# One core: a product of 512 bf16 columns into an unused bank behind each step's product of a tanh recurrence

## The reference

```
def _L0_attn_b_ref(x, A, B, C, gamma, beta):
    xb = jnp.einsum('bsd,ed->sbe', x, B)
    def step(h, xb_t):
        h = jnp.tanh(h @ A.T + xb_t)
        y = h @ C.T
        return (h, y)
    h0 = jnp.zeros((batch, d), dtype=x.dtype)
    _, ys = jax.lax.scan(step, h0, xb)
    out = jnp.transpose(ys, (1, 0, 2)) + x
    mu = jnp.mean(out, axis=-1, keepdims=True)
    var = jnp.mean(jnp.square(out - mu), axis=-1, keepdims=True)
    return (out - mu) * jax.lax.rsqrt(var + LN_EPS) * gamma + beta
...
x = x + _L0_attn_b_ref(_layernorm(x, axis=-1), L0_attn_b_A, ...)
```

## Time and profile before

| | |
|---|---|
| median of 3 runs | 6355.99 us (6347.57 to 6366.04) |
| the profiled execution, its own time | 6365.01 us |
| its span, first to last instruction | 6363.1 us |
| TensorE's mean granted clock over the span | 0.891 |
| the recurrence, from the first product to the last tanh | 2491.9 to 2753.4 us of the span |

### The profile page before, as it was taken

How to read it: one execution, slowest core, us unless ns; L and a number is a source line. 1 busy time by engine, 2 the same in 40 slices (tenths; PEclk the granted TensorE clock), 3 DMA queues, 4 the chain that set the end, 5 groups by cost and what they waited for, 6 DMA issues and landing times. The chain is left out here.

```text
span 6363.1 us, 79030 instructions
## 1 busy us (share of the span) xinstructions
PE 5155.9 (81%) x22250; PEld 2583.2 (41%) x22314; DVE 4310.5 (68%) x6171; ACT 2866.6 (45%) x4845; POOL 3250.2 (51%) x2383
## 2 busy tenths in 40 slices
PE   4888888888886897778977999954897799974897
PEld 1333333333332343534433555422664344442564
DVE  4999999999998474054765777752675566652675
ACT  4665665655654354233543555521332344431232
POOL 2788888888886252023523444317333455526333
PEclk8999999999999897578988999966998899986898
DMA  1224211211211000000002333222454333302455
GB/s 71 80 99 146 102 56 78 80 55 79 80 60 53 0 0 0 0 0 0 0 7 55 87 84 83 52 81 74 159 189 139 81 90 92 90 1 72 152 187 177
DMA packets 175518, 476.34 MB, mean 75 GB/s; under 512 B 29888, under 2 KB 55232, under 8 KB 147392
## 3 DMA queue, kind: packets, MB, share of 16 engines
q1 hardware_dynamic: 156992, 434.35, 21.4%
q0 software_dynamic: 18176, 37.79, 1.7%
HBM read 364.94 MB, written 107.07 MB: 74 GB/s over the span
## 5 line engine op out<-in xcount | busy, mean ns | idle before, releaser
L337 POOL TENSOR_TENSOR mamba_bu<-mamba_du,mamba_b_all 128x1024 f32<-128x1024 f32 x512 | 1200.3, 2355 | 282.5 <-DVE mamba_hc L599 270.2
L592 DVE TENSOR_TENSOR_SCAN mamba_bu<-psum,mamba_bu 128x512 f32<-128x512 f32 x1024 | 1194.2, 1208 | 157.6 <-ACT psum L529 124.9
L428 PE MATMUL psum<-mamba_hc,consts 128*128 128x512 f32 x2048 | 1019.0, 622 | 31.7 <-DVE mamba_du L604 28.6
L529 ACT ACTIVATE psum<-mamba_delta,A 128x510 f32<-128x510 f32 x1024 | 684.6, 685 | 571.4 <-DVE mamba_bu L592 556.8
L599 DVE TENSOR_TENSOR mamba_hc<-mamba_bu,psum 128x1024 f32<-128x1024 f32 x512 | 612.9, 1197 | 6.5 <-PE psum L419 4.5
L1597 POOL DMA_INDIRECT results<-ffn_moe_y_rows,ffn_moe_row_of x312 | 302.1, 968 | 506.3 <-DVE ffn_moe_y_rows L1787 430.7
L428 PEld LDWEIGHTS psum<-mamba_hc,consts 128*128 128x128 f32 x2048 | 404.2, 199 | 371.3 <-issue 351.0
L1712 ACT ACTIVATE ffn_moe_act<-ffn_moe_act 128x512 f32<-128x512 f32 x344 | 217.0, 631 | 719.9 <-DVE ffn_moe_act L1756 719.8
L2140 POOL TENSOR_TENSOR loc_q_bd<-loc_q_max,weights_l1a 128x512 fp32r<-128x512 f32 x256 | 274.8, 1102 | 416.8 <-DVE loc_q_max L2376 409.1
L419 PE MATMUL psum<-mamba_parts,consts 128*128 128x512 bf16 x448 | 177.6, 396 | 329.3 <-DVE mamba_hc L599 327.1
L2367 DVE TENSOR_REDUCE cau_top<-psum 128x2 f32<-128x512 f32 (+1 forms) x384 | 263.3, 692 | 212.0 <-PE psum L2207 198.8
(11 more groups left out here) (405 smaller groups left out, 11343.4 us busy)
## 6 DMA issues: line engine op xcount, KB each, us to landing
mamba_b_all<-b_rows SPq DMA_DIRECT2D x128, 1024.0 KB, 8.2
ffn_moe_w_gu<-gate_up_parts SPq DMA_DIRECT2D x78, 1024.0 KB, 4.8
pairs<-empty_rows SPq DMA_DIRECT2D x6, 3432.0 KB, 15.4
ffn_moe_got<-pairs SPq DMA_DIRECT2D x78, 264.0 KB, 3.2
ffn_moe_w_down<-in_l_moe SPq DMA_DIRECT2D x78, 256.0 KB, 2.9
qk_rows<-loc_qk SPq DMA_DIRECT2D x16, 1024.0 KB, 8.4
ffn_moe_back<-results SPq DMA_DIRECT2D x32, 512.0 KB, 4.8
qk_rows<-cau_qk SPq DMA_DIRECT2D x16, 1024.0 KB, 4.3
```

Source lines behind the costliest of these rows:

```text
L337: nc.gpsimd.tensor_tensor(bu[:, J % BU, :, :], du[:, q % 2, :, :], b, ALU.mult).then_inc(bu_ready, 1)
L428: nc.tensor.matmul(ysum[h], mem.ident, hc[:, J % HC, h, :], start=(n == 0), stop=(n == NST - 1), skip_group_check=True).then_inc(summed, 1)
L529: nc.scalar.activation(by_seq(dA[i % DECAYS])[:, :, 1:S], by_seq(delta[:, q % 2, h, :])[:, :, 1:S], ACT.Exp, scale=mem.A[:, q % 2, h * NST ...
L592: nc.vector.tensor_tensor_scan(bu[:, J % BU, h, :], dA[i % DECAYS], bu[:, J % BU, h, :], 0.0, ALU.mult, ALU.add).then_inc(scanned, 1)
```

## The change

One line is added in `chunk`, behind the step's product: a product of 512 bf16 columns, the identity by the masks, into bank 7, for each of the 256 steps. It waits for nothing and raises nothing, and nobody reads bank 7 in this stage. In TensorE's stream it stands between the product of step k and the wait for the tanh of step k; at k = 7 it stands ahead of the product of `inputs`.

More of the change, by code:

```diff
@@ L1146, in chunk @@
                                      skip_group_check=True).then_inc(pre_ready, 1)
+                    nc.tensor.matmul(mem.bank[7].rearrange("p (a k) -> p a k", a=4), mem.ident16, mem.masks, start=True, stop=True, skip_group_check=True)
             pe.wait_ge(input_ready, 1 + LEAD)
```

## The result

The change makes the kernel faster: 6319.65 us (median of 6 runs, 6313.66 to 6332.63) against 6354.06 us (median of 6, 6346.94 to 6366.04) before. The ratio is 0.9949, with a 95% interval of 0.9935 to 0.9963, so it is 0.5% faster: 34 us less, where 36 were forecast. The profiled execution has a span of 6330.8 us against 6363.1. TensorE's mean granted clock over the whole program was 0.905 in it, and 0.905 to 0.908 over the six runs.

A forecast was written before the change was run, and what follows sets the result against it. The recurrence was taken as bound by product and tanh in turn, at clock 0.50. Terms of 32.4 and 5.5 us less and 2.4 more sum to 35.5 less: 6329.5 profiled, 6320 for the median, range 6298 to 6350.

The forecast's parts named there:

- The bound and the cover: Recurrence, plain cold step: the added product costs 0, streaming from some 0.52 to 0.95, with 0.18 us of cover.
- The ring of product and tanh: Recurrence: product 0.64 us, tanh 0.20, next weight load 0.05 later; 0.92 us start to start at clock 0.50.
- the price ahead of `inputs` at 0.50: Interval with `inputs`: nothing covers the added product there, so it grows by 0.27 us; nine such intervals, 2.4 us more.
- The table-load interval: Where ScalarE loads its table between two tanhs (7 times): stays 1.68 us, the added product costs nothing.
- The price of the clock in a plain step: Plain step at clock 1.00: 0.70 us, 0.225 less; 8 x 18 such steps give 32.4 us less.
- The path of the clock: Recurrence: dense runs at `inputs` raise the clock, table loads let it fall; 18 of 29 plain steps per chunk pair warm.
- rival 1: Plain steps of the recurrence don't hold the warm clock; some 4 warm steps per chunk, 10 us less, 6346; chance 0.15.
- The term of `inputs`: Warm interval with `inputs`: 1.21 us instead of 2.13, 0.92 less; six of them give 5.5 us less.
- The upper end of 66 us: Largest gain, were all of the recurrence at full clock: 233 x 0.225 + 15 x 0.92 us.
- Rival 2: Recurrence clock never rises; the added product then costs 15 x 0.27 = 4 us, 6360; chance 0.09.
- Rival 3: The table load doesn't let the clock fall; nearly all of 66 us less, but for the first chunk, 6294; chance 0.07.
- Rival 4: Added product still in the array when the tanh is done; next step 0.18 us late, 42 more, 6398; chance 0.05.

The follow-up runs named there:

- both versions with pieces: Product of `inputs` cut into 8 pieces behind steps 8 to 15: alone in the kernel before, recurrence 240.2 us; with added columns and table loaded once, 178.2 us, ratio 0.9879.

## Why the prediction was right

**The bound and the cover.** Right. The ring of product and tanh set the stage, an added product of 128 rows cost a plain cold step nothing (0.92 with it and without), and the price ahead of `inputs` at 0.50 was +0.27 as forecast: 2.40 against 2.13. The table-load interval stayed 1.68. The cover is larger than forecast: the added product starts 0.44 into the cold step (2516.53 against 2516.09), where the prediction had 0.52.

**The price of the clock in a plain step.** Right: 0.225 less was worked out from products of 8 columns, 0.23 was measured (0.925 to 0.695). It was forecast for 144 plain steps; 137 ran wholly at 1.00 and 7 more had the clock change in them. Plain steps together are 32.7 us shorter; the term said 32.4.

**The path of the clock.** Right in part, both in what raises it and in what lowers it. Plain cold steps never raised it; all seven rises stand at or just behind an `inputs`. But two of the nine dense runs that came in the cold state did not raise it, the first and the last of them, so that steps 0 to 22 and 222 to 255 all ran at 0.50. The falls were put down to the table load. Five of seven stand there; the run with the table loaded once shows that they come without it as well. So rival 1 was right in part: warm steps with 512 columns don't hold the clock for good. I had taken 18 warm steps of 29 instead of 20 for that; the number was a choice and not worked out from a row, and that it came so near is luck.

**The term of `inputs`.** Wrong. "A product of 512 f32 columns takes 2.08 at 0.50 and 1.12 at 1.00, 0.96 less" took its warm price from a product of the layer norm that reads neighbouring columns. `inputs` reads at a stride of 1 KB, and at 1.00 it took 1.88: the warm interval is 2.07 and not 1.21, 0.06 less than before and not 0.92. The experiment with neighbouring columns gives 1.21. The price of the added product was carried over from 0.50 as well: at 1.00 the interval with `inputs` is 2.07 with it and 1.92 in the run that leaves it out there, so it costs 0.15 and not 0.27. The counts were as forecast, six warm and nine cold, but the 15 intervals are 1.6 us longer in all, where the forecast had 3.1 less. That is the whole difference between the 31.1 of the stage and the 35.5 of the sum. The upper end of 66 us was too high for the same reason, by 13.

**The median.** That 6319.65 lies within 1 us of the forecast 6320 is luck. The stage gave 31.1 of the 35.5 forecast. The medians differ by 34.4; the 3.3 beyond the stage's gain lie within the 19 us over which the repeats spread.

**The levels of the clock.** The spacing of small products is 0.213 at 0.50 and 0.11 at 1.00. What the Trainium skill's page "TensorE: Matmul & The Clock Gate" (section "Terms") says of the throttle, half the rate where the full clock isn't granted, agrees with that.

**The rivals.** Rival 2 (never rises) is what 256 columns give, but for one short rise. Rival 3 (nearly the whole stage warm) is what 768 columns give. Rival 4 is what 32 rows give. The change stands between them, and small edits tip it to either side.

## What to carry to other kernels

In a latency-bound ring on TensorE, look at the granted clock before the instructions: a stage at 0.50 pays for it in each product on its ring, here 0.64 us instead of 0.41. Idle time of the engine could be filled here up to the point where the next product could stream anyway. Filled with unused columns it bought the clock, and filled with work that is due anyway (the pieces of `inputs`) it bought that as well. Size the fill by trying more of it (512 columns lost the clock seven times, 768 twice), and don't put it where the engine is the bound. Price a product from a row that reads memory in the same pattern.

## What the runs showed of the hardware that was not expected

- An f32 product whose moving operand has a stride of 1 KB streams 512 columns in 0.85 us per record at a granted clock of 1.00 and at 0.50 (0.84 and 0.86 between records). With neighbouring columns it takes 0.43 at 1.00 and 0.85 at 0.50. So at 0.50 the stride can't be seen.
- A product on 32 rows between products on 128 rows didn't overlap with them: its weight load waits (0.56 behind the step's product instead of 0.23), and so does the next one. The same product on 128 rows is free, this one costs 0.18 us a step.
- With 512 added columns and the table loaded once the clock falls in steps that look all alike, after 17 to 31 us at 1.00; with 768 it doesn't fall. Why the stretches differ in length stays open.
- In both versions with pieces the intervals behind step 7 of chunks 0, 1 and 14, which are written out and not in the loop, are 0.06 to 0.07 longer than the others. The cause stays open.
